# Moving four exponents, two row copies and two powers in the front of a fused attention and mixture-of-experts kernel

## The reference

```python
def _L0_attn_ref(x, Wr, Wk, Wv, Wo, decay, gn_weight, gn_bias):
    r = jax.nn.sigmoid(jnp.einsum('btd,ed->bte', x, Wr))
    k = jnp.einsum('btd,ed->bte', x, Wk)
    v = jnp.einsum('btd,ed->bte', x, Wv)
    d = jax.nn.sigmoid(decay)
    log_decay = jnp.log(jnp.clip(d, 1e-07, None))
    pos = jnp.arange(T, dtype=x.dtype)
    scale = jnp.exp(pos[:, None] * log_decay[None, :])
    scaled = k * v / jnp.clip(scale, 1e-10, None)[None]
    state = jnp.cumsum(scaled, axis=1) * scale[None]
    out = r * state
    mean = jnp.mean(out, axis=(1, 2), keepdims=True)
    var = jnp.mean(jnp.square(out - mean), axis=(1, 2), keepdims=True)
    normed = (out - mean) * jax.lax.rsqrt(var + GN_EPS)
    normed = normed * gn_weight + gn_bias
    return jnp.einsum('btd,ed->bte', normed, Wo)
...
x = x + _L0_attn_ref(_layernorm(x, axis=-1), ...)
x = x + _L0_ffn_ref(_layernorm(x, axis=-1), ...)
```

## Time and profile before

| what | value |
|---|---|
| median of 3 runs | 691.92 us (691.54 to 692.03) |
| the profiled execution | 692.17 us, span 690.4 us |
| mean granted TensorE clock | 0.994 |
| PE busy | 661.1 us (96%) |
| DVE busy | 312.6 us (45%) |
| ACT busy | 163.7 us (24%) |
| POOL busy | 220.6 us (32%) |

### The profile page before, as it was taken

The page is one execution under the profiler, slowest core; times in us unless marked ns, Lnnn a source line. Parts: engine busy times, 40 slices in busy tenths (PEclk is TensorE's granted clock), DMA queues, the critical chain, the costliest instruction groups (busy, mean ns, idle before and its releaser), DMA issues. The chain is left out here.

```text
span 690.4 us, 8874 instructions
## 1 busy us (share of the span) xinstructions
PE 661.1 (96%) x3201; PEld 393.4 (57%) x3201; DVE 312.6 (45%) x742; ACT 163.7 (24%) x277; POOL 220.6 (32%) x210
## 2 busy tenths in 40 slices
PE   8989999999999998999999999999999999999992
PEld 7678878888878753444444454445444444544430
DVE  5787567778858772232223232323323222332321
ACT  5842215642211411111111111112112111111210
POOL 5566456435648121022121230203221122212112
PEclk9999999999999999999999999999999999999997
DMA  8210006613779879999999999999999999999963
GB/s 316 88 61 1 1 30 228 247 60 120 276 281 338 294 288 362 402 404 405 386 401 398 360 401 390 403 361 394 386 404 385 369 385 396 395 399 363 398 195 43
DMA packets 53627, 203.95 MB, mean 295 GB/s; under 512 B 7877, under 2 KB 8261, under 8 KB 53200
## 3 DMA queue, kind: packets, MB, share of 16 engines
q1 hardware_dynamic: 37504, 170.06, 61.9%
q0 software_dynamic: 9072, 21.52, 13.1%
q10 hardware_dynamic: 7008, 11.80, 4.5%
HBM read 179.48 MB, written 24.13 MB: 295 GB/s over the span
## 5 line engine op out<-in xcount | busy, mean ns | idle before, releaser
L690 POOL DMA_INDIRECT out_dram<-ym,midx x32 | 51.4, 1605 | 282.2 <-DVE ym L1293 141.9
L1660 PE MATMUL bank<-w_sb,xT 128*64 128x384 f32 x768 | 129.1, 489 | 0.8 <-ACT xT L922 0.8
L1433 PE MATMUL bank<-x_hi,w_parts 128*128 128x512 f32 x368 | 113.6, 391 | 2.5 <-ACT row_b L832 2.3
L1660 PEld LDWEIGHTS bank<-w_sb,xT 128*64 128x64 f32 x768 | 53.0, 137 | 71.0 <-issue 67.7
L1433 PEld LDWEIGHTS bank<-x_hi,w_parts 128*128 128x128 f32 x368 | 69.0, 188 | 17.4 <-issue 2.6
L1228 DVE TENSOR_TENSOR sg<-sg,bank 128x384 f32<-128x384 f32 x32 | 17.8, 555 | 116.3 <-issue 72.5
L1433 PE MATMUL bank<-x_lo,w_parts 128*128 128x512 f32 x184 | 70.2, 389 | 0.0
L1578 PE MATMUL bank<-sh_sb,xS 128*128 128x384 f32 x208 | 69.2, 486 | 0.0
L1681 PE MATMUL bank<-w_sb,guT 128*64 128x512 f32 x288 | 65.9, 592 | 1.1 <-DVE ym L1293 1.1
L1578 PEld LDWEIGHTS bank<-sh_sb,xS 128*128 128x128 f32 x208 | 38.7, 191 | 24.1
L949 ACT ACTIVATE y<-bank,wcol 128x512 fp32r<-128x512 f32 x26 | 17.9, 687 | 121.3 <-PE bank L1681 121.3
(11 more groups left out here) (191 smaller groups left out, 918.9 us busy)
## 6 DMA issues: line engine op xcount, KB each, us to landing
w_sb<-in_L_ffn_w_down SPq DMA_DIRECT2D x48, 768.0 KB
w_sb<-in_L_ffn_w_gate SPq DMA_DIRECT2D x48, 768.0 KB
w_sb<-in_L_ffn_w_up SPq DMA_DIRECT2D x48, 768.0 KB
extra<-in_L_ffn_w_gate SPq DMA_DIRECT2D x16, 768.0 KB
extra<-in_L_ffn_w_up SPq DMA_DIRECT2D x16, 768.0 KB
extra<-in_L_ffn_w_down SPq DMA_DIRECT2D x16, 768.0 KB
ring<-in_L_attn_x SPq DMA_DIRECT2D x14, 256.0 KB, 3.7
xS<-xt_dram SPq DMA_DIRECT2D x13, 256.0 KB
```

Source lines behind the costliest of these rows:

```text
L690: pool.indirect_dma_start(out=out[:, :], out_offset=bass.IndirectOffsetOnAxis(ap=midx[j % 3][u][:, :], axis=0), in_=ym[u][:, :], in_offset ...
L1433: ins = pe.matmul(ps[u][:, :], w, xp, start=(n == 0), stop=(n == len(parts) - 1))
L1660: ins = pe.matmul(ps[e * C:(e + 1) * C, 0:I], xT[:, c, e * C:(e + 1) * C], gate_up(2 * j + u, e, k)[:, c, :], start=(c == 0), stop=(c == K ...
```

## The change

Three edits, one on each of three engines. On GpSimd two more `low` run ahead of the powers of tiles 4 and 5, and two behind. On ScalarE the copy of `row_w` goes between the scale exponentials and those of the inverse, and that of `row_b` behind the inverse's, ahead of step 0. On VectorE exponents 0 and 1, with the multiply of 4 columns that they need, go ahead of tiles 4 and 5; exponents 2 and 3 stay behind these tiles. No instruction is added or taken out.

```diff
@@ GpSimd
             low(2, 1)
+            low(0, 2)
+            low(2, 2)
             powers(2)
-            for c in range(2, KC):
-                low(0, c)
-                low(2, c)
+            low(0, 3)
+            low(2, 3)
             powers(1)
@@ ScalarE
             def output_weights():
-
-                act.wait_ge(rows_ready, 1)
-                act.activation(row_w[:, :], ps_t[1][:, :], ACT.Copy).then_inc(rows_copied, 1)
-                act.wait_ge(rows_ready, 2)
-                act.activation(row_b[:, :], ps_k[1][:, :], ACT.Copy).then_inc(rows_copied, 1)
                 act.wait_ge(vectors_in, 16 * 2)
                 act.wait_ge(raw_in[3], 16)
...
             for c in range(KC):
                 act.activation(scale[:, c, :], pos_i[:, :], ACT.Exp, scale=dec[:, 3, c:c + 1]).then_inc(setup, 1)
+            act.wait_ge(rows_ready, 1)
+            act.activation(row_w[:, :], ps_t[1][:, :], ACT.Copy).then_inc(rows_copied, 1)
             for c in range(KC):
                 act.wait_ge(power_ready, c + 1)
                 act.activation(inv[:, c, :], inv[:, c, :], ACT.Exp).then_inc(inv_made, 1)
+            act.wait_ge(rows_ready, 2)
+            act.activation(row_b[:, :], ps_k[1][:, :], ACT.Copy).then_inc(rows_copied, 1)
             for s in range(STEPS):
                 step(s)
@@ VectorE
+            dve.wait_ge(setup, 3)
+            seq.then(dve.tensor_scalar(dec[:, 4, :], dec[:, 3, :], -1.0, None, ALU.mult))
+
+            def exponents(c):
+                dve.tensor_scalar(inv[:, c, :], pos_i[:, :], dec[:, 4, c:c + 1], MOST,
+                                  ALU.mult, ALU.min).then_inc(power_ready, 1)
+
+            exponents(0)
+            exponents(1)
             for n in (4, 5):
                 x_stats(n)
             for n in (4, 5):
                 x_norm(n)
-            dve.wait_ge(setup, 3)
-            seq.then(dve.tensor_scalar(dec[:, 4, :], dec[:, 3, :], -1.0, None, ALU.mult))
-            for c in range(KC):
-                dve.tensor_scalar(inv[:, c, :], pos_i[:, :], dec[:, 4, c:c + 1], MOST,
-                                  ALU.mult, ALU.min).then_inc(power_ready, 1)
+            exponents(2)
+            exponents(3)
```

## The result

The changed kernel takes 694.22 us in the median of 16 runs (691.05 to 699.58), the kernel before 692.35 us (691.02 to 697.08, 16 runs beside it). The ratio is 1.0034, with a 95% interval of 1.0021 to 1.0047: 2.3 us slower by the ratio, 1.9 us by the two medians. The forecast was no measurable difference, 692.4 us, in a range of 690.7 to 693.7. The profiled execution took 694.14 us with a span of 692.3, against 692.17 and 690.4 before.

The account below looks back on a forecast made before the run. TensorE, busy for 96% of the span, was taken to bound the kernel. Its stalls summed to -2.25 + 2.73 = +0.48 us, giving 692.4 us on the median of 691.92, in a range of 690.7 to 693.7.

Parts of the forecast that it names:

- Both gates hang on ScalarE: TensorE's stall on `row_b` goes (-2.25 us); its wait on `x_lo` before tile 6 grows from 0.97 to 3.70 us.
- The turns of VectorE and GpSimd: Both engines alternate by whole instructions; exponents 0 and 1 run free, 2 and 3 end at 29.6 and 30.3 us.
- rival B: On VectorE, exponents 2 and 3 end early, by 27.7 and 28.4; -1.5 us, 690.4 us; chance 0.11.
- The idle time of ScalarE moves between exponentials 1 and 2: Inverse exponential 2 waits for its exponent until 29.63; number 3 ends at 31.65, as before (31.70).
- `row_b` goes onto the chain: ScalarE's copy stands ahead of the table load, delaying it 0.48 us and tile 6's start to 40.63 from 40.15.
- rival D: TensorE's 3.7 us stall lowers its clock, slowing step 2's products: +2.8, in sum +3.3 us, 695.2 us; chance 0.07.
- C: Both TensorE stalls shrink and ScalarE's idle 2.6 us go wholly; -1.9 us, 690.1 us; chance 0.04.
- E: Copies between ScalarE's exponentials call for up to two table loads of 1.28 us; +2.6 us, 695.0 us; chance 0.02.

Follow-up runs that it names:

- copies alone: Only ScalarE's edit (row_w ahead of the inverse's exponentials, row_b behind them) on the kernel before, VectorE and GpSimd untouched; ratio to before 1.0031.
- broken gap: Changed kernel with 4 unused transposes on TensorE between tiles 5 and 6, released when v of step 1 is copied; ratio to before 1.0030, median 692.72 us.
- six_later: Changed kernel with tile 6 transposed behind step 2 and no longer behind step 1; median 691.17 us, ratio to before 0.9993.
- stats_early: Changed kernel with tile 7's statistics and power taken ahead of step 0, tile 6 staying behind step 1; median 694.12 us, ratio to before 1.0025.
- both_on_before: Kernel before, with tile 6 transposed behind step 2 and tile 7's statistics and power ahead of step 0; median 691.55 us, ratio to before 0.9992.

## Why the prediction was wrong

*Both gates hang on ScalarE, and the second one takes over:* right. The stall on `row_b` went and came back at tile 6, 3.52 us in one piece against 3.70 forecast.

*The turns of VectorE and GpSimd:* right in order, a little off in time. The changed kernel has them on the two engines as follows:

```profile
20.44 1.23 DVE L1157 TENSOR_SCALAR dec<-dec 128x4 f32<-128x4 f32 x1
21.71 1.42 DVE L1160 TENSOR_SCALAR inv<-pos_i,dec 128x1024 f32<-128x1024 int32 x2
...
26.13 1.42 DVE L1019 TENSOR_SCALAR xn<-xin,mv,rstd 128x512 f32<-128x512 f32 x1 [0.52 <-POOL rstd L555]
27.48 2.44 DVE L1160 TENSOR_SCALAR inv<-pos_i,dec 128x1024 f32<-128x1024 int32 x2
...
18.24 1.73 POOL L566 TENSOR_TENSOR w_parts<-wr_raw,w_parts 128x512 fp32r<-128x512 f32 x1
19.93 1.72 POOL L566 TENSOR_TENSOR w_parts<-wk_raw,w_parts 128x512 fp32r<-128x512 f32 x1
26.00 1.27 POOL L566 TENSOR_TENSOR w_parts<-wr_raw,w_parts 128x512 fp32r<-128x512 f32 x1
27.24 1.47 POOL L566 TENSOR_TENSOR w_parts<-wk_raw,w_parts 128x512 fp32r<-128x512 f32 x1
```

The 4-column multiply waits out a `low` (ends 21.67, I had 22.05), two exponents run free in 1.42, tile 5 is behind `low(0,3)`, and exponent 2 behind `low(2,3)`, so rival B was rightly held small.

*The idle time of ScalarE moves between exponentials 1 and 2, and `row_b` goes onto the chain:* right, and here is where the size was off:

```profile
25.33 1.99 ACT L866 ACTIVATE inv<-inv 128x1024 f32<-128x1024 f32 x2
29.29 2.01 ACT L866 ACTIVATE inv<-inv 128x1024 f32<-128x1024 f32 x2 [1.97 <-DVE inv L1160]
31.20 0.58 ACT L868 ACTIVATE row_b<-bank 128x512 f32<-128x512 f32 x1
31.80 1.28 ACT L747 ACT_TABLE_LOAD   x1
```

Number 2 started at 29.29 in place of 29.63, since the front ran 0.1 us early and each turn was somewhat shorter than I added up. The table load is 0.09 us later than before, not 0.48, and the gate +0.11. The copies alone, in an execution that started as before (scale exponentials at 20.81 against 20.79), gave +0.52 and +0.53, which is the forecast's size. Of the 0.4 us between, 0.1 is the earlier start of this execution, and the rest is about what the earlier exponents won back by themselves (0.3 us above).

*The clock:* this is the step that failed: the sum put the cost of the longer stall at nothing beyond its length, and the clock that fell behind it cost 1.57 us. I saw that the change makes one stall of 3.7 us out of two, wrote it down as rival D with a chance of 0.07, and left it out of the sum. My ground was that 3.7 us lies between a gap that kept the clock (2.25) and about 5 us that lost it. The 5 us were read wrongly. From 677.65 to about 682.8 is the time until the clock was low, and an upper end for the idle time that it takes, no more: in the changed kernel it fell at 41.7, also 5 us after TensorE went idle (36.75), although TensorE was at work again since 40.26; with the copies alone it fell 4.1 us after (40.8 for 36.7), with the broken gap 2.7 us after (39.2 for 36.5). And the broken gap shows that the length of one stall is not enough as a measure. Between two ends with nothing in between, a chance near 0.5 would have been honest; 0.07 was worked out from no row. The price of D was too large: I doubled a group of 2.83 us, and the clock was low for 3.4 us, worth 1.57. With the measured gate and this price the sum is +1.7, and 692.35 + 1.7 = 694.0 against 694.22 measured.

By the Trainium skill, page "TensorE: Matmul & The Clock Gate", section "Why this matters for your kernels", gaps of a few microseconds are to be avoided between bursts. The trace of the changed kernel agrees, at 3.52 us. The broken gap isn't covered by that rule: there the longest stall was 1.48 us and the clock fell too.

Rivals B, C and E didn't come: exponent 2 started behind `low(2,3)`, the second gate stood, and the two copies among the exponentials needed no table load.

## What to carry over

A wait that TensorE loses nothing by moving isn't free to move: two short stalls apart can be cheaper than their sum in one piece, as the clock falls behind the long one, and here it cost 1.6 us where the removed wait brought nothing. When one stall is taken out, look for the next gate on the same chain first, and move that gate's consumer (here the transpose of one tile) or shorten its chain; then the first edit begins to count. If neither can be done, work of no use on TensorE in the gap can hold the clock: here 28 transposes did and 4 did not. The kernel before already runs such transposes of `ident` between those of its first tiles (line 1504).

## What the runs showed of the hardware

In each of the five profiled executions in which the clock fell in the front (the changed kernel, the broken gap, the copies alone, *six_later* and *stats_early*), it was low for 3.4 us. It fell 2.7 to 5.0 us after TensorE had gone idle. In four of them TensorE was back at work by then, for 0.1 to 1.4 us, so the slow matmuls stand behind the stall and not in it. The loss from tile 6 to tile 7 was 1.57 to 1.61 us where the whole low stretch fell on work (changed kernel, copies alone, *stats_early*), and 1.19 us with the broken gap. A longest stall of 1.48 us (broken gap) and one of 2.39 us (*six_later*) had the clock fall behind them, one of 2.25 us (before) and one of 2.21 us (*both_on_before*) did not; what tells them apart stays open. Four f32 transposes in the middle of the gap didn't prevent it, 28 that filled it did. In the rows of the front, VectorE's exponents and multiplies and GpSimd's `low` take turns by whole instructions, and the one already waiting goes first: a multiply of 4 columns took 1.23 us and ended at 21.67, with GpSimd's `low` ending at 21.65.
